# VectorE sums the second layer's weighted rows over their slots, and layer 1's last steps follow one round sooner

## What is computed

```python
# layer 0
vals, idx = top_k(where(A != 0, -arange(N), -inf), 25)
agg = where(valid, X[idx], -inf).max(axis=2)
agg = where(degree <= 25, maximum(agg, 0), agg)
x = layernorm(x + relu(concat([X, agg]) @ W + b))
# layer 1
Wh = (x @ W1).reshape(..., 8, 32)
e = s1[:, :, None] + s2[:, None] + edge_emb[adj]
e = where(e > 0, e, 0.2 * e);  e = where(adj == 0, -1e9, e)
alpha = softmax(e, axis=2)
h = einsum('bijh,bjhd->bihd', alpha, Wh)      # the sum that the change moves
h = layernorm_affine(h);  h = elu(h)
x = layernorm(x + h)
```

## Time and profile before

| | us |
|---|---|
| median of 3 runs | 3497.86 (3492.01 to 3498.03) |
| the profiled execution's own time | 3493.1 |
| its span, from its first to its last instruction | 3491.4 |
| mean granted clock of TensorE | 0.687 of 2.4 GHz |
| busy: PE / PEld | 1589.2 / 1182.6 |
| busy: DVE | 2372.5 |
| busy: ACT | 1115.7 |
| busy: POOL | 2515.1 |

### The profile page before, as it was taken

How to read it: one execution, slowest core, us unless ns; L and a number is a source line. 1 busy time by engine, 2 the same in 40 slices (tenths; PEclk the granted TensorE clock), 3 DMA queues, 4 the chain that set the end, 5 groups by cost and what they waited for, 6 DMA issues and landing times.

```text
span 3491.4 us, 25323 instructions
## 1 busy us (share of the span) xinstructions
PE 1589.2 (46%) x5123; PEld 1182.6 (34%) x5131; DVE 2372.5 (68%) x5655; ACT 1115.7 (32%) x2307; POOL 2515.1 (72%) x2640
## 2 busy tenths in 40 slices
PE   0045456344453444544365344554444443655544
PEld 0033334233332333333243233433333332444433
DVE  8797787665677667777597665867665543755466
ACT  3223344333343323433344232332222211233134
POOL 2576777777777777777777776777777777777675
PEclk9976567666676666666676666766676666767776
DMA  6667777655576555765567555564434443444332
GB/s 229 220 200 255 263 251 231 208 182 178 165 238 194 183 178 187 256 202 187 164 221 252 186 187 156 175 194 150 147 109 123 116 115 106 120 117 114 96 107 75
DMA packets 220561, 614.24 MB, mean 176 GB/s; under 512 B 66801, under 2 KB 110834, under 8 KB 193778
## 3 DMA queue, kind: packets, MB, share of 16 engines
q0 software_dynamic: 124416, 346.88, 33.4%
q1 hardware_dynamic: 95986, 265.69, 22.5%
HBM read 559.43 MB, written 52.95 MB: 175 GB/s over the span
## 4 chain that ended last, share of the span: by engine, by line
POOL 61%; issue 22%; DVE 8%; PE 4%; DMA 2%; DVEq 2%; ACT 1%; POOLq 0%; SPq 0%; ACTq 0%
POOL ring L549 53%; POOL sorted_d L527 4%; POOL out_dram L564 3%; DVE cand L970 2%; PE att_p L828 2%; DVEq L931 2%; DVE agg L1080 1%; DMA ring<-table_d,idx_loc 1%; POOL table_d L557 1%; DVE adj_h L966 1%; PE lin_p L792 1%; DVE ring L1234 1%; DVE agg L1073 0%; DMA ring<-sorted_d,idx_cur 0%; DMA ring<-in_x_dram,top_cur 0%
## 5 line engine op out<-in xcount | busy, mean ns | idle before, releaser
L549 POOL DMA_INDIRECT ring<-table_d,idx_loc x1128 | 1081.0, 958 | 396.3 <-issue 340.7
L549 POOL DMA_INDIRECT ring<-sorted_d,idx_cur x705 | 677.0, 960 | 214.9 <-issue 214.9
L800 PE MATMUL score_p<-ident,x1k 128*128 128x128 f32 x256 | 81.3, 419 | 1477.4 <-ACT x_t L638 1473.5
L1080 DVE TENSOR_REDUCE agg<-ring 128x256 f32<-128x2560 f32 (+9 forms) x120 | 453.1, 3776 | 344.4 <-DMA ring<-sorted_d,idx_cur 244.9
L828 PE MATMUL att_p<-ring,ident 128*128 128x256 f32 (+1 forms) x2384 | 607.9, 414 | 153.1 <-DVE ring L1234 153.1
L828 PEld LDWEIGHTS att_p<-ring,ident 128*128 128x128 f32 (+1 forms) x2384 | 500.0, 211 | 257.0 <-DVE ring L1234 158.5
L800 PEld LDWEIGHTS score_p<-ident,x1k 128*128 128x128 f32 x256 | 35.9, 197 | 1528.1 <-issue 1523.7
L669 ACT ACTIVATE neg<-z 128x256 f32<-128x256 f32 x128 | 53.3, 416 | 1430.1 <-DVE z L1123 1423.1
L549 POOL DMA_INDIRECT ring<-in_x_dram,idx_cur x423 | 404.0, 955 | 134.6 <-issue 128.0
L792 PE MATMUL lin_p<-w_s,h_t 128*128 128x256 f32 x1024 | 474.9, 644 | 0.0
L792 PEld LDWEIGHTS lin_p<-w_s,h_t 128*128 128x128 f32 x1024 | 320.9, 328 | 149.2 <-issue 81.0
(11 more groups left out here) (152 smaller groups left out, 2775.5 us busy)
## 6 DMA issues: line engine op xcount, KB each, us to landing
adj_i<-in_adj_dram SPq DMA_DIRECT2D x208, 1024.0 KB, 5.8
ring<-table_d,idx_loc POOLq DMA_INDIRECT x1128, 2.8
pay<-in_x_dram SPq DMA_DIRECT2D x8, 2048.0 KB, 10.0
xs<-sorted_d SPq DMA_DIRECT2D x128, 128.0 KB, 5.7
ring<-sorted_d,idx_cur POOLq DMA_INDIRECT x705, 2.9
table_d<-tab SPq DMA_DIRECT2D x80, 132.0 KB, 3.4
ring<-in_x_dram,idx_cur POOLq DMA_INDIRECT x423, 3.5
sorted_d<-pay,rank_i POOLq DMA_INDIRECT x128, 3.6
```

The lines of the kernel that those rows point to most:

```text
L549: pool.indirect_dma_start(out=to[:, k * width:(k + 1) * width], out_offset=None, in_=source, in_offset=bass.IndirectOffsetOnAxis(ap=idx_at ...
L1080: last = v.tensor_reduce(a, rows.rearrange("p (k c) -> p c k", c=C), AX, ALU.max)
```

## The change

DVE takes over the sum over the slots. Right behind the weighting of a tile, in the same round, it adds the rows with one TENSOR_REDUCE into `att_s`; for the heavy tile it takes two and an add for the 32 nodes with more than 16 slots. `attend` on TensorE, `copy_att` on ScalarE and the semaphores `weighted` and `att_copied` go. `att_ready`, for which GpSimd waits before it overwrites a part of the ring, is now incremented by DVE. All that follows for the tile comes one round sooner on DVE and ScalarE: statistics at j - 1, layernorm and ELU at j - 2, `res` at j - 3; GpSimd scatters tile j - 4, and there is one round less.

```diff
-LAG1 = 5
-ROUNDS = TILES + LATER + 4
+LAG1 = 4
+ROUNDS = TILES + LATER + 3
...
-            def copy_att(j):
-                act.wait_ge(att_ready, j + 1)
-                act.activation(att_s[j % 2][:, :], att_p[:, 0:C], ACT.Copy).then_inc(att_copied, 1)
...
                 if first(j - 2):
-                    copy_att(j - 2)
-                if first(j - 3):
-                    elu(j - 3)
+                    elu(j - 2)
...
-            def attend(j):
-                u = tile1(j)[1]
-                k = SLOTS[u]
-                pe.wait_ge(weighted, j + 1)
-                need(pe, att_copied, j)
-                rows = ring_tile(1, j)
-                r3 = rows.rearrange("p (k c) -> p k c", c=ROW)
-                for s in range(k):
-                    on = P if u or s < FULL else TOPS
-                    last = pe.matmul(att_p[:, 0:C], ident[0:on, :], r3[0:on, s, 0:C],
-                                     start=(s == 0), stop=(s == k - 1))
-                last.then_inc(att_ready, 1)
...
-                i2, i3, j2, j3, j4 = r - 2, r - 3, j - 2, j - 3, j - 4
+                i2, i3, j1, j2, j3 = r - 2, r - 3, j - 1, j - 2, j - 3
...
-                if first(j4):
-                    need(dve, final_out[j4 % 4], 16 * (j4 // 4))
-                    normal(res[j4 % 4][:, :], y2[:, :], 2).then_inc(final_ready, 1)
+                if first(j3):
+                    need(dve, final_out[j3 % 4], 16 * (j3 // 4))
+                    normal(res[j3 % 4][:, :], y2[:, :], 2).then_inc(final_ready, 1)
...
                     v.tensor_tensor(g4[:, 0:w], g4[:, 0:w], p3[:, 0:w, :].unsqueeze(3)
-                                    .broadcast_to([P, w, H, DH]), ALU.mult).then_inc(weighted, 1)
+                                    .broadcast_to([P, w, H, DH]), ALU.mult)
+                    settle()
+                    to = att_s[j % 2]
+                    last = v.tensor_reduce(to[:, :], g3[:, 0:w, 0:C].rearrange("p k c -> p c k"), AX, ALU.add)
+                    if u == 0:
+                        v.tensor_reduce(rprod[0:TOPS, 0:C], g3[0:TOPS, FULL:, 0:C].rearrange("p k c -> p c k"),
+                                        AX, ALU.add)
+                        settle()
+                        last = v.tensor_tensor(to[0:TOPS, :], to[0:TOPS, :], rprod[0:TOPS, 0:C], ALU.add)
+                    last.then_inc(att_ready, 1)
```

More of the change, by code:

```diff
@@ L294, in build @@
         exp_ready = sem("exp_ready")
-        weighted = sem("weighted")
         att_ready = sem("att_ready")
-        att_copied = sem("att_copied")
         z2_ready = sem("z2_ready")
@@ L839, in _ @@
                 j = r - LATER
-                if first(j - 1):
-                    attend(j - 1)
                 g = sorted_in(r - 2)
@@ L1113, in steps @@
                     v.reciprocal(rstd[:, :], std[:, :])
-                if first(j3):
-                    v.scalar_tensor_tensor(z2[:, :], att_s[j3 % 2][:, :], mv[:, 2:3], gam[:, :],
+                if first(j2):
+                    v.scalar_tensor_tensor(z2[:, :], att_s[j2 % 2][:, :], mv[:, 2:3], gam[:, :],
                                            ALU.subtract, ALU.mult)
@@ L1172, in steps @@
                         .then_inc(logits_ready, 1)
[L1173 to L1178, removed]
+                if first(j1):
+                    att = att_s[j1 % 2][:, :]
+                    b1, u1 = tile1(j1)
+                    if u1 == T - 1:
+                        q = b1 % 3
                         v.tensor_scalar(att, att, has[:, 2 * q:2 * q + 1], None, ALU.mult)
                         settle()
-                        dve.wait_ge(mean_ready, b2 + 1)
+                        dve.wait_ge(mean_ready, b1 + 1)
                         v.scalar_tensor_tensor(att, mean_wh[:, :], has[:, 2 * q + 1:2 * q + 2], att,
                                                ALU.mult, ALU.add)
-                if first(j3):
-                    dve.wait_ge(elu_ready, j3 + 1)
+                if first(j2):
+                    dve.wait_ge(elu_ready, j2 + 1)
                     v.scalar_tensor_tensor(y2[:, :], z2[:, :], 0.0, neg[:, :], ALU.max, ALU.add)
-                if first(n) or first(j3) or first(j2):
+                if first(n) or first(j2) or first(j1):
                     settle()
@@ L1196, in steps @@
                                            ALU.max, ALU.add).then_inc(z_ready, 1)
+                if first(j1):
+                    v.bn_stats(stats[:, 6:12], att)
                 if first(j2):
[L1198 to L1201, removed]
+                    b2, u2 = tile1(j2)
+                    v.scalar_tensor_tensor(y2[:, :], y2[:, :], -1.0, x1_at(b2 * T + u2), ALU.add, ALU.add)
                 settle()
@@ L1209, in steps @@
                 settle()
-                for x, there in enumerate((i2, j2, j3)):
+                for x, there in enumerate((i2, j1, j2)):
                     if first(there):
```

## The result

The changed kernel takes 3567.58 us (median of four runs, 3566.86 to 3568.32) against 3496.91 us before (median of four, one more than in the table above): a ratio of 1.0198, with a 95% interval of 1.0183 to 1.0214, or 71 us more. Forecast were 3566 us, between 3518 and 3603.

What follows compares the result with a forecast made beforehand. The prediction took GpSimd's back-to-back indirect DMA issues to set the pace. Light stretches +51 us, TensorE's sums -2 and the end +19 made +68, so a median of 3566 us, between 3518 and 3603.

Steps and rivals of the forecast that it cites:

- Bound and mechanism: POOL's back-to-back DMA issues set the pace; added DVE time stops POOL in the light stretches and at the end.
- DVE hides it all: Rival: DVE's idle time covers all the added reduces, so the kernel gets faster, 3484 us; chance 0.05.
- light stretches: Rounds with r mod 16 from 7 to 11, gathering only 13 to 14 slots, where DVE has no time to spare.
- The price of the reduce: DVE's new slot sums: 1.66 ns an element, 0.22 us fixed each, 540 us of DVE time in all.
- The upper end: Margin on the cost of DVE's reduce: 1.8 ns an element, for layer 1's row pitch of 1056 bytes, not 1024.
- The rival of 1.04 ns: Rival: DVE's reduces take 1.04 ns an element, 330 us in all, giving +21 us, 3519; chance 0.05.
- The leads: Light stretches: 19.1 us of reduces less the time from res to its scatter (11.5, 4.9, 6.4, 3.8) delays POOL; +51 us.
- The rank sums: In light stretches, DVE's wait for TensorE's rank sums (3.8 us each) hides the 1.9 us reduce of 4 slots.
- TensorE's sums gone: At POOL's nine ring waits for `att_ready`, DVE's sum frees POOL 0.9 us sooner in one; -2 us for all nine.
- The end: Last graph: reduces from 11 to 4 slots cost 24.5 us more, less one closing round of 5.95 us; +19 us.
- The closing round: At the end of the kernel, one round without gathers falls away, saving 5.95 us.
- TensorE's clock: If TensorE is granted a lower clock, layer 0's `lin_p` is used a round later and hides it; 0 us.

Runs made afterwards that it cites:

- e9: The changed kernel without the reduces for tiles u = 0 and 12 to 15 of the first seven graphs; 3512.13 us.
- e10: The changed kernel with reduces only for tiles u = 0, 1 and 12 to 15 of the first seven graphs; 3536.03 us.
- e4: The changed kernel with TensorE's matmuls kept at their old places, writing a result nobody reads from a constant tile; 3566.13 us.
- e11: The kernel before plus a DVE reduce whose result nobody reads, over rows 1024 bytes apart instead of 1056; 3579.46 us.
- e7: The changed kernel with a maximum in place of the sum in the new reduce L1214; 3564.36 us.

## Why the prediction was right

**Bound and mechanism: right.** The page's chain, POOL's unchanged issue time and the stretch with no idle time on either engine gave the place, and e9 and e10 show it by leaving out one side and then the other. The rival "DVE hides it all" is out by 84 us. Its error is the average: DVE still idles 633 us after the change, and for 388 of them it waits for rows, outside the light stretches with the search.

**The price of the reduce: a little low.** 540 us were forecast, 534.7 + 30.3 = 565 measured, since the rate is 1.79 and not 1.66 ns an element. The upper end, 1.8 for the longer pitch, had it. The rival of 1.04 ns, the Trainium skill's one element a cycle ("VectorE: DVE Perf Modes", section "The perf-mode tier table"), falls: no strided reduce over SBUF here ran at it, neither max nor add.

**The leads: the sum right, its parts less so.** Forecast for the first five stretches were 7.6, 14.2, 12.7, 15.3 and 4, less 3; measured are 4.4, 19.7, 17.0, 12.4 and 0.1, in all 53.6 against 51. The single leads were read from one round each, and POOL's waits on res are five small ones per stretch (16.2, 17.1 and 15.0 us in the second to the fourth), as the leads of its other rounds are short too. In the first stretch the step was wrong in kind: the lead of 11.5 us to the scatter of res held (0.5 us of waits), and POOL stopped at the table's scatter, a hand-over that the prediction did not look at. In the fifth POOL waits 4.7 us for res and waits 2.2 less for the ring before it (6.7 after 8.9). The rank sums did cover the tile of 4 slots: L973's waits fell from 26.6 to 16.1 us. In the third stretch alone they did not fall (2.4 before, 2.7 after); there e9, with no reduce in this place, waits 4.6, and the difference to 2.7 is the reduce's 1.9 us.

**TensorE's sums gone: nothing gained.** -2 us were forecast for the nine ring waits. With the one that changed its name they went from 55.6 to 54.9 us: some 4 us less in the first six graphs, 2.8 more at the turn, where two heavy tiles follow each other as the prediction feared. Two new waits of 1.8 us before layer 0's heavy tile, put down to "issue", take back more than that. The step that failed is the price of one wait, 0.9 us. It set the end of DVE's sum, 1710.5, against the start of POOL's gather, 1711.40, but POOL starts 0.76 us behind the end of the sum with either engine: TensorE's matmuls end at 1710.64 in the profile. And DVE's sum of 13 slots takes 6.10 us, not 5.75. In the changed kernel, the gather of the earlier trace rows one graph on its way:

```profile
1725.33 3.62 DVE L1210 TENSOR_TENSOR ring<-ring,score_p 128x3328 f32<-128x3328 f32 x1
...
1729.02 6.10 DVE L1214 TENSOR_REDUCE att_s<-ring 128x256 f32<-128x3328 f32 x1
...
1735.88 0.95 POOL L547 DMA_INDIRECT ring<-table_d,idx_loc  x1 [7.78 <-DVE att_s L1214]
```

From the end of the weighting to the gather these are 6.9 us, and 6.7 with TensorE. So DVE's sum was no sooner there than TensorE's.

**The end: right in sum, by two misses.** Behind the fifth stretch 53.6 us were lost and 73.9 at the end, 20.3 for the last graph with its turn, where +19 was forecast for the end. Of these, 8.3 come before round 138, at the turn and in the last graph's heavy tiles, where the forecast had next to nothing. The thirteen rounds from 11 to 4 slots lost 18.1, not 24.5: their reduces took 47.5 us, but all 38.6 us of waits for rows went, of which the forecast counted 32.5. The closing round gave back 6.1, forecast 5.95. DVE's waits from 3385 to 3550 us:

```profile
DVE y L1162 <- ACT neg L665: 9.0, 13, 0.9
```

Rows are not among them any more: DVE runs behind in all these rounds, and the ELU's answer costs it 0.7 us in each, near the 1 us that was allowed.

**TensorE's clock: right to leave out.** The granted clock fell from 0.687 to 0.594, towards the lower of its two levels (0.5, or 1.2 GHz) once the sums were gone, and e4 shows that this cost nothing that can be measured (3566.13 with 0.684, 3567.58 with 0.594).

Against the forecast of 3566 stand 3567.58 us, or +71 against +68. That the two are so near owes something to errors that cancel: the first, fourth and fifth stretch were put 3.2, 2.9 and 3.9 us too high, the second and third 5.5 and 4.3 too low, and the end's two parts miss in opposite directions. The place and the kind of the loss were foreseen; its parts were known to some 5 us each.

## What to carry to other kernels

Two engines that take turns at setting the pace look idle on the page, each by its average. Cut the span at the stages and ask of each what the engine that is to get the work has to spare there, and how far the other may run ahead of it; the lead of a hand-over, read from two rows of the timeline, says how much may be added before a wait appears. Every hand-over of the stretch has to be read so, not only the one that looks nearest: in the first stretch here another one gave way. A step put a round closer has to be paid by the latency that the round hid, and the places where a ring wraps can be worth more than its size.

## What the runs showed of the hardware

A TENSOR_REDUCE in fp32 over slots that lie a row apart in SBUF took 1.66 ns an element at 1024 bytes of pitch (max, layer 0), 1.71 (add, e11) and 1.79 at 1056 bytes (add in L1214 and max in e7 alike). From PSUM, with 32 bytes of pitch, the kernel's own L1223 took (350 - 232)/112 = 1.05 ns between 80 and 192 elements (below 80 its times do not lie on a line). L1165, a max of the same shapes and the same pitch over `e` in SBUF, took (488 - 288)/112 = 1.79, so the faster rate goes with PSUM here and not with the short step; add against max made no difference in e7. Both are of the kernel before:

```profile
L1223 DVE TENSOR_REDUCE su<-score_p 128x8 f32<-128x80 f32 x16 | 3.7, 232 | 0.0
...
L1223 DVE TENSOR_REDUCE su<-score_p 128x8 f32<-128x192 f32 x8 | 2.8, 350 | 0.0
...
L1165 DVE TENSOR_REDUCE mx<-e 128x8 f32<-128x80 f32 x16 | 4.6, 288 | 0.4
...
L1165 DVE TENSOR_REDUCE mx<-e 128x8 f32<-128x192 f32 x8 | 3.9, 488 | 0.2
```

GpSimd's indirect DMAs took 0.96 us beside 565 us more of these reduces, as before. In the changed kernel the 274 gathers whose issue lies wholly inside one of the new reduces took 0.948 us on average and the other 2,014 took 0.960, so the reduces did not slow them.
